# Attention scores by query: diagonal blocks in tiles of their own, one wide mask product per head, and the slots of a unit laid out anew

## The chip, the cores and the metric

The kernel runs as one program on one core of a Trainium2 chip. The time is device microseconds of one execution, median of several; lower is better. The engines are named as the profile names them: PE is TensorE's matmul row, PEld its weight loads, DVE is VectorE, ACT is ScalarE, POOL is GpSimd, SP issues the DMAs.

## The reference, cut to what matters

Six layers follow each other on x of 8 sequences x 512 positions x 128 features: a mixture of experts, an RWKV layer, the mixture again, a second mixture (top 1 of 8), causal attention, and the second mixture again. The change touches the attention alone:

```python
qkv = jnp.einsum('bsm,qhkm->qbhsk', x, w_qkv)          # 16 heads of 8
scores = jnp.einsum('bhsk,bhtk->bhst', Q, K) / sqrt(d_k)
scores = jnp.where(causal, scores, -jnp.inf)
probs = jax.nn.softmax(scores, axis=-1)
attn = jnp.einsum('bhst,bhtk->bhsk', probs, V)
x = x + einsum('bsd,md->bsm', attn_cat, w_o)
```

Here S is 512, in 4 blocks of 128.

## The kernel before, in words

The attention works through 8 sequences ("batches", functions `body(b, ...)`) of 4 units each. A unit (b, g) is 4 heads. Each head's q and k lie in 32 rows of a stack (`q_stack`, `k_stack`), so that a product of one head uses 32 of the 128 rows of PE, and products of different heads can run beside each other. The scores of a unit are computed twice:

- By query (`by_query`, PE lines 2019 and 2023), only to find each query's maximum. Six tiles n = 0..5 per unit, of two heads each, in PSUM banks 0 to 3, two tiles in flight. Before, a tile holds whole causal rows of a query block i: (i + 1) * 128 keys. Where the block touches the diagonal, a product of the identity with the constant `keys_after` (0 or -1e30, bf16, all 128 rows of PE, L2023) is added on its last 128 columns. n = 0, 1 hold block 3 (512 columns), n = 2, 3 hold block 2 (384) and block 0 (128), n = 4, 5 hold block 1 (256). DVE takes the maxima (`maxima`, L1490).
- By key (`by_key`, L2006), 12 tiles t = 0..11 per unit of one head each (t is called a slot), in banks 4 and 5 by turns: width 512 for t = 0..3, 384 for t = 4..7, 256 + 128 for t = 8..11. ACT takes their exponentials (`exps`, L938), POOL clears what lies beyond the diagonal (L620), and PE multiplies with the values one unit later (`weighted_values`, L2036, fp32, columns of PE in four groups of 32), in four parts j = 0..3 at slots 1, 3, 5, 5.

The maxima go by a transpose (`max_rows`, L1995), a copy on ACT (L945) and a DMA into the q stack of the unit, ahead of its by-key scores. `by_query` and `maxima` therefore run two units ahead of `by_key`.

The order on each engine is written out by hand in `body`: in each slot, weighted values, then `by_key(t)`, then in even slots `by_query(u + 2, ..., t // 2)`, then other work put at a slot: transposes of the weighted values (`transpose_values`, L2043, slot 8), which need ACT's copy `values` (L950); in unit g = 0 the projections of the next batch, `q_proj` at slot 6 and `k_proj` at slot 10 (L1590 to L1592, both into bank 7); `v_proj` in g = 1; in g = 2 `transpose_out` (L2049) at slot 6 and `out_proj` at slot 10, both in bank 7 too; in g = 3 the transposes of the next layer's input (L1580). `k_proj` waits for `q_low` of DVE (L1475), which waits for `q_high` of ACT (L925), since they empty bank 7. `out_proj` waits for `out_low` of DVE (L1507), which waits for `out_high` of ACT (L960), in the same way. `by_key(t)` waits for the exponential of slot t - 2 (semaphore `probs_ready`), `by_query(n)` for the maxima of tile n - 2 (`scores_by_query_used`).

## Time and profile before

| | |
|---|---|
| median of 3 runs | 1802.65 us (1800.73 to 1805.01) |
| the profiled execution | 1796.81 us, span 1794.7 us, mean granted clock 0.98 |
| attention | from 1374 to about 1715 us of the span |
| one batch of 4 units | 38.8 to 39.1 us where the clock stays up |
| PE busy, DVE busy over the span | 94%, 68% |

PE's busy time counts the whole latency of a matmul (a 128 column one is shown with 219 ns, though in a run of them one starts every 56 ns), so a busy PE may still be waiting in part. In the views of order of time, the first number is the start, the second the length of the group of like instructions, and a bracket tells the idle time before it and what ended it. A unit is found by its `by_key` matmuls of 512 columns on L2006.

### The profile page before, as it was taken

To read this page: it belongs to the slowest core of one execution; us is meant where nothing else is said; L and a number is where in the kernel's file an instruction comes from. 1 tells how busy PE (TensorE), PEld (TensorE's weight loads), DVE (VectorE), ACT (ScalarE), POOL (GpSimd) and SP (SyncE) were. 2 spreads that over 40 slices of the span, in tenths; PEclk is the share of its full clock that TensorE was granted. 3 is DMA by queue.
4 is the path that set the end of the run, shared out by engine and by line. 5 is a ranking of instruction groups with operands and counts; after the bars stand their busy time and mean duration, and the time that the engine had idled before them with its cause. 6 is when DMAs were issued, how large, how long until landed. Compare 5 with 4: busy or idle time off the path is not lost. (4 is left out here: it accounts for less than half of the span.)

```text
span 1794.7 us, 45173 instructions
## 1 busy us (share of the span) xinstructions
PE 1691.7 (94%) x15966; PEld 1000.2 (56%) x15966; DVE 1226.7 (68%) x2848; ACT 1017.1 (57%) x1956; POOL 876.7 (49%) x722
## 2 busy tenths in 40 slices
PE   7899999999998999979999999999999998999988
PEld 4566666666665666646666666666644343434334
DVE  5865666666667888746665665666678786888566
ACT  5655555555555566545555555566533775777633
POOL 2665765665541435556755655765443222232232
PEclk9999999999999999999999999999999998999889
DMA  4200000000000000000000000000001110111000
GB/s 144 85 20 1 0 0 0 0 0 1 2 1 2 2 0 0 2 1 1 2 1 0 0 0 0 0 1 1 2 1 25 28 37 15 43 28 25 2 13 35
DMA packets 14617, 23.41 MB, mean 13 GB/s; under 512 B 2570, under 2 KB 10890, under 8 KB 14356
## 3 DMA queue, kind: packets, MB, share of 16 engines
q1 hardware_dynamic: 14484, 21.62, 4.2%
q8 instruction: 85, 1.39, 0.3%
q14 instruction: 48, 0.39, 0.1%
HBM read 11.00 MB, written 2.10 MB: 7 GB/s over the span
## 5 line engine op out<-in xcount | busy, mean ns | idle before, releaser
L506 POOL TENSOR_TENSOR scratch<-scratch 128x512 f16<-128x512 f32 x384 | 445.5, 1160 | 416.6 <-ACT scratch L667 416.3
L667 ACT ACTIVATE scratch<-scratch 128x512 f16<-128x512 f32 x512 | 322.4, 630 | 440.7 <-DVE scratch L1110 440.6
L1110 DVE SCALAR_TENSOR_TENSOR scratch<-psum,scratch 128x512 f32<-128x512 f32 x512 | 352.9, 690 | 313.8 <-ACT scratch L662 180.1
L1628 PE MATMUL psum<-ffn_down_hi,scratch 128*128 128x128 f16 x2048 | 369.3, 219 | 2.5 <-POOL scratch L506 2.1
L1630 PE MATMUL psum<-ffn_down_hi,scratch 128*128 128x128 f16 x2048 | 369.2, 219 | 0.0
L1629 PE MATMUL psum<-ffn_down_lo,scratch 128*128 128x128 f16 x2048 | 369.2, 219 | 0.0
L662 ACT ACTIVATE scratch<-psum 128x512 f32<-128x512 f32 x512 | 296.7, 580 | 0.0
L1490 DVE TENSOR_REDUCE scratch<-psum 128x2 f32<-128x1024 f32 (+3 forms) x256 | 202.4, 822 | 56.7 <-PE psum L2023 53.5
L1628 PEld LDWEIGHTS psum<-ffn_down_hi,scratch 128*128 128x128 f16 x2048 | 200.3, 98 | 60.4 <-POOL scratch L506 3.1
L1629 PEld LDWEIGHTS psum<-ffn_down_lo,scratch 128*128 128x128 f16 x2048 | 200.4, 98 | 56.1
L1590 PE MATMUL psum<-x_hi,ffn_up_hi 128*128 (+1 forms) x512 | 195.7, 382 | 7.8 <-DVE scratch L1110 7.6
L1630 PEld LDWEIGHTS psum<-ffn_down_hi,scratch 128*128 128x128 f16 x2048 | 200.4, 98 | 0.0
L1590 PE MATMUL psum<-x_hi,ffn_gate_hi 128*128 (+1 forms) x512 | 194.7, 380 | 3.6 <-ACT scratch L662 2.7
L1591 PE MATMUL psum<-x_lo,ffn_up_hi 128*128 (+1 forms) x512 | 195.1, 381 | 0.0
L1592 PE MATMUL psum<-x_hi,ffn_up_lo 128*128 (+1 forms) x512 | 195.0, 381 | 0.0
L1591 PE MATMUL psum<-x_lo,ffn_gate_hi 128*128 (+1 forms) x512 | 194.8, 380 | 0.0
L1592 PE MATMUL psum<-x_hi,ffn_gate_lo 128*128 (+1 forms) x512 | 194.7, 380 | 0.0
L499 POOL TENSOR_TENSOR scratch<-e_const,scratch 128x16 f32<-128x16 f32 x56 | 163.4, 2917 | 0.0
L480 POOL TENSOR_TENSOR ln_rstd<-ln_var,neg_half 128x4 f32<-128x4 f32 x48 | 48.5, 1010 | 210.8 <-DVE ln_var L1030 210.8
L1125 DVE SCALAR_TENSOR_TENSOR x_tok<-psum,scratch,x_tok 128x128 f32 (+1 forms) x512 | 143.2, 343 | 5.3 <-DVE scratch L1100 2.9
L938 ACT ACTIVATE scratch<-psum 128x384 f32<-128x384 f32 x256 | 116.3, 490 | 43.0 <-PE psum L2006 41.7
L1117 DVE TENSOR_TENSOR scratch<-scratch 128x512 f16<-128x512 f32 x128 | 88.8, 694 | 52.6 <-ACT scratch L667 50.1
(225 smaller groups left out, 2861.6 us busy)
## 6 DMA issues: line engine op xcount, KB each, us to landing
raw<-in_ffn_w_dram SPq DMA_DIRECT2D x8, 768.0 KB, 4.5
scratch<-scratch SPq DMA_DIRECT2D x32, 128.0 KB, 2.7
ffn_up_hi<-scratch SPq DMA_DIRECT2D x32, 128.0 KB, 2.7
x_tok<-in_x_dram SPq DMA_DIRECT2D x8, 256.0 KB, 6.7
out_dram<-x_tok SPq DMA_DIRECT2D x8, 256.0 KB, 2.0
raw<-in_lin_dram SPq DMA_DIRECT2D x1, 1092.0 KB
half_sb<-in_half_dram SPq DMA_DIRECT2D x1, 544.0 KB, 5.7
con_sb<-in_con_dram SPq DMA_DIRECT2D x1, 410.5 KB, 5.1
```

The lines of the kernel that those rows point to most:

```text
L499: pool.tensor_tensor(lg_exp[:, c], e_const[:], lg_shift[:, c], ALU.pow).then_inc(s_exp, 1)
L506: pool.tensor_tensor(h_lo[r], h32[r], h_hi[r], ALU.subtract).then_inc(s_plo, 1)
L662: act.activation(gate_act[k % 2], bank(k % 2), ACT.Silu, scale=W_DOWN).then_inc(s_s, 1)
L667: act.activation(h_hi[k % HSLOTS], h32[k % HSLOTS], ACT.Copy).then_inc(s_hhi, 1)
L1110: dve.scalar_tensor_tensor(h32[k % HSLOTS], bank(5 + k % 2), W_DOWN, gate_act[k % 2], ALU.mult, ALU.mult).then_inc(s_h, 1)
L1490: ins = dve.tensor_reduce(neg_max[g % 2][:, a:a + SUB + 1:SUB], scores[:, :, at:at + (i + 1) * P], AX_X, ALU.max, negate=True)
L1590: pe.matmul(dst, lhs[0], rhs[0], start=first, stop=False)
L1591: pe.matmul(dst, lhs[0], rhs[1], start=False, stop=False)
L1592: return pe.matmul(dst, lhs[1], rhs[0], start=False, stop=last)
L1628: pe.matmul(dst, h_hi[r][:, cols], hi, start=k % FC == 0 and n == 0, stop=False, skip_group_check=True)
L1629: pe.matmul(dst, h_hi[r][:, cols], lo, start=False, stop=False, skip_group_check=True)
L1630: ins = pe.matmul(dst, h_lo[r][:, cols], hi, start=False, stop=k % FC == FC - 1 and n == SUB - 1, skip_group_check=True)
```

## The change

`by_query` now knows three kinds of tile. Kind 0 holds the four diagonal blocks of two heads: 8 products of 128 columns, and then one mask product of 512 columns per head, whose moving operand is `keys_after` repeated four times by a step of zero. Kinds 1 and 2 (`LEFT`) hold what lies left of the diagonal, without a mask: kind 1 block 3 (384 columns) and block 1 (128), kind 2 block 2 (256). The six tiles of a unit are of the kinds 2, 0, 1, 1, 0, 2.

DVE reduces a tile of kind 0 in one instruction (8 maxima of 128) into `neg_max`, the left parts into a new tile `neg_left`, and after the last tile takes the minimum of both for blocks 1 to 3 (negated maxima), with a semaphore `maxima_ready` that `max_rows` waits for.

In `body`, the weighted values stand at slots 1, 4, 6, 6 (before 1, 3, 5, 5). On ACT `values` moves from slot 6 to 7, `q_high` from 7 to 8, `v_copy` from 9 to 10, `out_high` from 7 to 8, the copy of the next input from 9 to 10. On PE `v_proj` and the next input's transposes move from slot 8 to 9; `transpose_values` stays at slot 8, `q_proj`, `transpose_out` at 6, `k_proj`, `out_proj` at 10.

```diff
@@ query_tile @@
-            return (2, 0)[n % 2], ([(3, 0)], [(2, 0), (0, 3 * P)], [(1, 0)])[n // 2]
+            return (2, 0)[n % 2], (2, 0, 1, 1, 0, 2)[n]
+
+        LEFT = {1: [(3, 0), (1, 3 * P)], 2: [(2, 0)]}
@@ ACT, body @@
-                            if t == 7 and g == 0 and more:
+                            if t == 8 and g == 0 and more:
                                 q_high(b + 1)
...
-                            if t == 6 and not (first and g == 0):
+                            if t == 7 and not (first and g == 0):
                                 values(u - 1)
-                            if t == 9 and g == 1 and more:
+                            if t == 10 and g == 1 and more:
                                 v_copy(b + 1, 1 - odd)
-                            if t == 7 and g == 2 and not first:
+                            if t == 8 and g == 2 and not first:
                                 out_high(b - 1)
...
@@ DVE, maxima @@
-                    for i, at in pieces:
-                        a = r * SUB + i
-                        ins = dve.tensor_reduce(neg_max[g % 2][:, a:a + SUB + 1:SUB], scores[:, :, at:at + (i + 1) * P], AX_X, ALU.max, negate=True)
+                    if kind == 0:
+                        ins = dve.tensor_reduce(neg_max[g % 2][:, r * SUB:(r + 2) * SUB], by(psum[...], 2 * SUB),
+                                                AX_X, ALU.max, negate=True)
+                    else:
+                        for i, at in LEFT[kind]:
+                            a = r * SUB + i
+                            ins = dve.tensor_reduce(neg_left[g % 2][:, a:a + SUB + 1:SUB], scores[:, :, at:at + i * P], AX_X, ALU.max, negate=True)
                     ins.then_inc(s_p1used, 1)
+                    if n == QT - 1:
+                        dve.wait_ge(s_p1used, QT * u + QT + 2)
+                        whole, left = [by(t, HG)[:, :, 1:SUB] for t in (neg_max[g % 2], neg_left[g % 2])]
+                        dve.tensor_tensor(whole, whole, left, ALU.min).then_inc(s_mneg, 1)
@@ PE, max_rows @@
-                    pe.wait_ge(s_p1used, QT * (u + 1) + 2)
+                    pe.wait_ge(s_mneg, u + 1)
@@ PE, by_query @@
-                    for m, (i, at) in enumerate(pieces):
+                    if kind == 0:
+                        for i in range(SUB):
+                            for x in range(2):
+                                rows, block = head(first + x), slice(i * P, (i + 1) * P)
+                                pe.matmul(bank(2 * (n % 2) + x)[:, block], q_stack[odd][g][rows, block], k_stack[odd][g][rows, block],
+                                          start=i == 0, stop=False, skip_group_check=True)
                         for x in range(2):
...
+                            ins = pe.matmul(by(bank(2 * (n % 2) + x), SUB), ident_b, keys_after.rearrange("p (o k) -> p o k", o=1).to_broadcast([P, SUB, P]),
                                             start=False, stop=True, skip_group_check=True)
+                    else:
+                        for i, at in LEFT[kind]:
+                            for x in range(2):
+                                rows = head(first + x)
+                                ins = pe.matmul(bank(2 * (n % 2) + x, at, at + i * P), q_stack[odd][g][rows, i * P:(i + 1) * P], k_stack[odd][g][rows, 0:i * P],
+                                                start=True, stop=True)
@@ PE, body @@
-                PV_AT = (1, 3, 5, 5)
+                PV_AT = (1, 4, 6, 6)
-                            if t == 8 and g == 1 and more:
+                            if t == 9 and g == 1 and more:
...
                                 v_proj(b + 1)
```

The places at which the order of the instructions counts are taken from batch 5, which is written out without a loop. Lines of the changed kernel are shifted: `by_key` is L2018 there, the diagonal blocks L2032, the wide mask L2035, the left parts L2041, weighted values L2054, `max_rows` L2007, `transpose_values` L2061, the projections L1602 to L1604.

PE, unit g = 0, slots 1 to 4, before:

```order
L2006 MATMUL psum<-ffn_up_hi 128x512 x2
L2019 MATMUL psum<-ffn_up_hi 128x512 x2
L2023 MATMUL psum<-big_sb 128x128 x2
L1995 MATMUL psum<-con_sb,scratch 16x128
L2036 MATMUL psum<-scratch,ffn_down_hi 32x384 x4
L2006 MATMUL psum<-ffn_up_hi 128x512
L2006 MATMUL psum<-ffn_up_hi 128x384
L2019 MATMUL psum<-ffn_up_hi 128x384 x2
L2019 MATMUL psum<-ffn_up_hi 128x128 x2
L2023 MATMUL psum<-big_sb 128x128 x4
```

The weighted values (j = 1) stand right behind full-width work, and slot 4 ends in masks. The same slots now:

```order
L2018 MATMUL psum<-ffn_up_hi 128x512 x2
L2032 MATMUL psum<-ffn_up_hi 128x128 x8
L2035 MATMUL psum<-big_sb 128x512 x2
L2007 MATMUL psum<-con_sb,scratch 16x128
L2018 MATMUL psum<-ffn_up_hi 128x512
L2054 MATMUL psum<-scratch,ffn_down_hi 32x384 x4
L2018 MATMUL psum<-ffn_up_hi 128x384
L2041 MATMUL psum<-ffn_up_hi 128x384 x2
L2041 MATMUL psum<-ffn_up_hi 128x128 x2
```

The masks of the unit's first half have gathered in slot 2, `by_key(3)` stands alone between them and the weighted values, and slot 4 has none.

PE, unit g = 0, slots 5 to 8, before (L1590 to L1592 are `q_proj`):

```order
L2006 MATMUL psum<-ffn_up_hi 128x384 x2
L2019 MATMUL psum<-ffn_up_hi 128x384 x2
L2019 MATMUL psum<-ffn_up_hi 128x128 x2
L2023 MATMUL psum<-big_sb 128x128 x4
L1590 MATMUL psum<-x_hi,scratch 128x512
L1591 MATMUL psum<-x_lo,scratch 128x512
L1592 MATMUL psum<-x_hi,scratch 128x512
L2006 MATMUL psum<-ffn_up_hi 128x384
L2006 MATMUL psum<-ffn_up_hi 128x256
L2006 MATMUL psum<-ffn_up_hi 128x128
L2019 MATMUL psum<-ffn_up_hi 128x256 x2
L2023 MATMUL psum<-big_sb 128x128 x2
```

Slots 6 to 8 now, with the transposes of the weighted values as the last row:

```order
L2018 MATMUL psum<-ffn_up_hi 128x384
L2041 MATMUL psum<-ffn_up_hi 128x384 x2
L2041 MATMUL psum<-ffn_up_hi 128x128 x2
L1602 MATMUL psum<-x_hi,scratch 128x512
L1603 MATMUL psum<-x_lo,scratch 128x512
L1604 MATMUL psum<-x_hi,scratch 128x512
L2018 MATMUL psum<-ffn_up_hi 128x384
L2018 MATMUL psum<-ffn_up_hi 128x256
L2018 MATMUL psum<-ffn_up_hi 128x128
L2032 MATMUL psum<-ffn_up_hi 128x128 x8
L2035 MATMUL psum<-big_sb 128x512 x2
L2061 MATMUL psum<-con_sb,scratch 128x128 x4
```

Slot 6 has lost its four masks, and slot 8 holds a whole diagonal tile with 1024 columns of mask.

DVE, unit g = 0 from its first maxima to `k_low` of g = 1 (L1475 is `q_low`, L1497 and L1501 are `normalise`), before:

```order
L1490 TENSOR_REDUCE scratch<-psum 128x2 x7
L1475 SCALAR_TENSOR_TENSOR scratch<-psum,scratch 128x512
L1497 RECIPROCAL scratch<-psum 128x16
L1501 TENSOR_TENSOR scratch<-psum,scratch 128x4x32
L1490 TENSOR_REDUCE scratch<-psum 128x2 x2
L1479 SCALAR_TENSOR_TENSOR scratch<-psum,scratch 128x512
```

And now:

```order
L1498 TENSOR_REDUCE scratch<-psum 128x2
L1493 TENSOR_REDUCE scratch<-psum 128x8
L1498 TENSOR_REDUCE scratch<-psum 128x2 x4
L1493 TENSOR_REDUCE scratch<-psum 128x8
L1478 SCALAR_TENSOR_TENSOR scratch<-psum,scratch 128x512
L1509 RECIPROCAL scratch<-psum 128x16
L1513 TENSOR_TENSOR scratch<-psum,scratch 128x4x32
L1498 TENSOR_REDUCE scratch<-psum 128x2
L1503 TENSOR_TENSOR scratch<-scratch 128x4x3
```

The reduction right ahead of `q_low` is now a diagonal one of 1024 elements instead of one of 512, and each unit ends with the minimum (L1503).

## Rows read from the trace of the kernel before

**Rows 1.** Busy time by window: length, busy (count) per engine, granted clock, DMA.

```profile
1552.00:1591.00 39.00, 35.74 (x379) 16.09 (x378) 32.17 (x59) 27.95 (x62) 10.93 (x17) 1.00 0.13 29
1484.90:1495.00 10.10, 10.10 (x65) 3.36 (x65) 5.37 (x9) 3.93 (x9) 1.25 (x3) 0.50 0.01 2
```

**Rows 2.** Who waited for whom, 1552 to 1591 us: total us, times, longest.

```profile
DVE scratch L1490 <- PE psum L2023: 5.8, 12, 0.7
...
PE psum L2006 <- ACT scratch L938: 3.4, 7, 0.8
```

**Rows 3.** Order of time on PE, unit g = 0, slots 0 to 6.

```profile
1551.74 0.38 PE L2006 MATMUL psum<-scratch 32*128 32x512 f16 x1 [0.54 <-ACT scratch L938]
...
1552.27 0.28 PE L2023 MATMUL psum<-big_sb 128*128 128x128 bf16 x2
1552.48 1.06 PE L2036 MATMUL psum<-ffn_gate_lo,ffn_down_lo 128*32 128x512 f32 x8
1553.48 0.39 PE L2006 MATMUL psum<-scratch 32*128 32x512 f16 x2
1553.49 0.59 PE L2019 MATMUL psum<-scratch 32*128 32x512 f16 x2
1554.01 0.29 PE L2023 MATMUL psum<-big_sb 128*128 128x128 bf16 x2
1554.14 0.27 PE L1995 MATMUL psum<-con_sb,scratch 128*16 128x128 f32 x1
1554.34 0.85 PE L2036 MATMUL psum<-scratch,ffn_down_lo 128*32 128x384 f32 x8
1555.12 0.39 PE L2006 MATMUL psum<-scratch 32*128 32x512 f16 x2
...
1555.99 0.86 PE L2036 MATMUL psum<-scratch,ffn_down_lo 128*32 128x256 f32 x16
1556.78 0.33 PE L2006 MATMUL psum<-scratch 32*128 32x384 f16 x2
1556.78 0.54 PE L2019 MATMUL psum<-scratch 32*128 32x384 f16 x4
```

**Rows 4.** PE, slots 8 to 11, and the starts of units g = 1, g = 2 and g = 0.

```profile
1558.73 0.61 PE L2043 MATMUL psum<-con_sb,scratch 128*128 128x128 f32 x4
...
1560.45 0.28 PE L2006 MATMUL psum<-scratch 32*128 32x256 f16 x1 [0.84 <-ACT scratch L938]
...
1560.87 0.38 PE L1590 MATMUL psum<-x_hi,scratch 128*128 x1
1561.09 0.38 PE L1591 MATMUL psum<-x_lo,scratch 128*128 x1
...
1561.62 0.39 PE L2006 MATMUL psum<-scratch 32*128 32x256 f16 x2
...
1571.89 0.38 PE L2006 MATMUL psum<-scratch 32*128 32x512 f16 x1 [0.54 <-ACT scratch L938]
...
1590.93 0.37 PE L2006 MATMUL psum<-ffn_up_hi 32*128 32x512 f16 x1 [0.63 <-ACT scratch L938]
```

**Rows 5.** Order of time on ACT, unit g = 0.

```profile
1557.15 0.87 ACT L938 ACTIVATE scratch<-psum 128x384 f32<-128x384 f32 x2 [0.48 <-PE psum L2006]
1557.90 0.60 ACT L950 ACTIVATE scratch<-psum 128x512 f32<-128x512 f32 x1
...
1559.00 1.01 ACT L925 ACTIVATE scratch<-psum 128x1024 f16<-128x1024 f32 x1
```

**Rows 6.** Order of time on DVE, units g = 0 and g = 2.

```profile
1560.04 0.69 DVE L1475 SCALAR_TENSOR_TENSOR scratch<-psum,scratch 128x512 f16<-128x512 f32 x1 [0.41 <-ACT scratch L925]
...
1579.85 0.68 DVE L1507 TENSOR_TENSOR scratch<-psum,scratch 128x512 f16<-128x512 f32 x1
```

**Rows 7.** Groups of DVE by shape: busy, mean ns.

```profile
L1490 DVE TENSOR_REDUCE scratch<-psum 128x2 f32<-128x1024 f32 x8 | 9.8, 1226 | 3.7 <-PE psum L2023 3.7
...
L1030 DVE TENSOR_SCALAR ln_var<-ln_mv 128x4 f32<-128x4 f32 x48 | 9.3, 194 | 3.6
```

More of the change, by code:

```diff
@@ L208, in build @@
         neg_max = [carve(HG * SUB) for _ in range(2)]
+        neg_left = [carve(HG * SUB) for _ in range(2)]
         max_row = carve(P, F16)
@@ L983, in body @@
                                 k_high(b + 1)
-                            if t == 6 and not (first and g == 0):
+                            if t == 7 and not (first and g == 0):
                                 values(u - 1)
-                            if t == 9 and g == 1 and more:
+                            if t == 10 and g == 1 and more:
                                 v_copy(b + 1, 1 - odd)
-                            if t == 7 and g == 2 and not first:
+                            if t == 8 and g == 2 and not first:
                                 out_high(b - 1)
-                            if t == 9 and g == 3 and prep:
+                            if t == 10 and g == 3 and prep:
                                 prep_xT(n0 + SUB * b + LEAD, (b + 2) % NB if isinstance(b, int) else b + 2, 7)
@@ L2010, in by_query @@
                 def by_query(u, b, g, n, odd):
-                    first, pieces = query_tile(n)
+                    first, kind = query_tile(n)
                     if n == 0:
@@ L2015, in by_query @@
                     pe.wait_ge(s_p1used, QT * u + n + 1)
-                    for m, (i, at) in enumerate(pieces):
-                        for x in range(2):
-                            rows = head(first + x)
-                            pe.matmul(bank(2 * (n % 2) + x, at, at + (i + 1) * P), q_stack[odd][g][rows, i * P:(i + 1) * P], k_stack[odd][g][rows, 0:(i + 1) * P],
-                                      start=m == 0, stop=False, skip_group_check=True)
-                    for m, (i, at) in enumerate(pieces):
-                        for x in range(2):
-                            ins = pe.matmul(bank(2 * (n % 2) + x, at + i * P, at + (i + 1) * P), ident_b, keys_after,
-                                            start=False, stop=True, skip_group_check=True)
+                    if kind == 0:
[4 more added lines that the diff above has]
+                                          start=i == 0, stop=False, skip_group_check=True)
+                        for x in range(2):
+                            ins = pe.matmul(by(bank(2 * (n % 2) + x), SUB), ident_b, keys_after.rearrange("p (o k) -> p o k", o=1).to_broadcast([P, SUB, P]),
+                                            start=False, stop=True, skip_group_check=True)
+                    else:
[4 more added lines that the diff above has]
+                                                start=True, stop=True)
                     ins.then_inc(s_p1, 1)
@@ L2122, in body @@
                                 out_proj(b - 1)
-                            if t == 8 and g == 3 and prep:
+                            if t == 9 and g == 3 and prep:
                                 if more:
```

6 lines of the change are left out of this document (4 added, 2 removed).

## The prediction

> **What bounds the kernel now.** I read the page first, for its span, the engines' shares and the slices that hold attention. The change touches attention only, so everything below is a sum over its 341 us. Then the windows: in 39 us, one batch of four units, PE is busy 35.7, DVE 32.2 and ACT 28.0 us, at the upper of the two clocks [rows 1]. The order of time on PE shows that no engine is the bound all the way. PE works in its written order and stops wherever its next product waits for an exponential: 3.4 us of modelled idle in 7 stops per batch behind ACT's main group [rows 2]. A stop costs more than that number. PE is counted busy for the latency of its last matmul: a 128 column product is shown with 0.22 us where the next could start after 0.055, so I add 0.15 us for each of the 7, and have about 4.4 us of waits and 34.7 us of work in a batch of 39.1. DVE is rarely the one that is waited for; it waits 5.8 us per batch for masks [rows 2]. So the change is worth what it takes from PE's 34.7 us of work, less what it adds to the 4.4 us of waits.
>
> **Prices, all from rows.** A 128 column product costs PE 0.055 us: two masks and then `max_rows` stand 0.13 apart [rows 3]. A 512 column product costs 0.22 (1560.87 to 1561.09, [rows 4]). Going from products on 32 rows to products on 128, or to the weighted values on 32 columns, costs an empty 0.10: the first mask starts 1552.27, the second 0.055 later would be through at 1552.38, and L2036 starts at 1552.48 [rows 3]. I call that a switch. Weighted values with the switch behind them: 1.00 for j = 0, 0.78 for j = 1, 0.79 for j = 2 and 3 (1552.48 to 1553.48, 1554.34 to 1555.12, 1555.99 to 1556.78, [rows 3]). Products of different heads run together, those of one head one after the other: L2006 and L2019 start 0.01 apart, and the masks behind them 0.52 later, twice 0.216 and a switch [rows 3]. An exponential of 384 columns starts 0.37 after its product (1556.78 to 1557.15) and takes 0.49 [rows 3, 5].
>
> The four diagonal blocks of a head are four weight loads and products one after the other in the same 32 rows. The trace's nearest case is slot 6: each of two heads does 384 and then 128 columns in its own rows, and all four are over in 0.54 us [rows 3], which is 0.16 for the product of `by_key` ahead of one of them, 0.16, 0.055 and the latency of 0.16, and leaves nothing for an exposed load. So I take 0.22 for the four blocks. The Trainium skill speaks against it: "TensorE: Matmul & The Clock Gate", Part 3, section The mechanism, says that a weight load overlaps running products only where its row group differs. By that rule each block after the first would wait for its load; the trace does not show it for two products in a row, and none here has four.
>
> **The work on PE, before and after.** The columns of a unit are the same: 5120 of scores, 2048 of masks. Masks in 4 products of 512 instead of 16 of 128 cost 0.86 us instead of 0.88. The switches of a unit are 15 before (six from row products into masks, six back, three from masks to weighted values) and 14 now (in and out of three places of weighted values, which stand between row products, and of four full-width ones): -0.10. The row products overlap better. Before, each mask cut them in six runs of 0.38, 0.43, 0.43, 0.38, 0.27, 0.27, 2.15 us. Now a unit g = 0 has 0.27, 0.43, 0.22, 0.22, 0.22, 0.38, 0.27 = 2.0, units without other work in slot 6 0.2 less. Together 0.3 to 0.5 us of work goes per unit, 1.65 us per batch: 33.0 us are left.
>
> **The waits, unit g = 0 of the changed order, from the start of `by_key(0)`.** Row products 0.22, switch, j = 0: `by_key(1)` at 1.31 and (3) at 2.48 after diagonal blocks (to 1.75), switch, masks 0.43, `max_rows` 0.11, switch. `by_key(4)` at 3.58, (6) at 4.68, `q_proj` 0.65 and two switches, (7) and (8) at 5.73. Until there nothing waits for over 0.1. The blocks and masks of slot 8 end at 6.64 and the transposes come next. They need `values`, which now stands behind the exponential of slot 7: product 5.73, exponential 6.10, `values` 6.48 to 7.08. Before, it was behind that of slot 6 and ended at 1558.50 against transposes at 1558.73 [rows 4, 5]. New wait 0.5. Transposes 0.44 and a switch: `by_key(9)`, (10) at 7.68, not waiting; here the 0.84 us stop before slot 10 is gone [rows 4]. They end at 7.95, `k_proj` is next. It needs `q_high` (1.01) and `q_low` (0.69) [rows 5, 6]. `q_high` follows the exponential of slot 8 and ends at 8.36, `q_low` 9.09. Before, `q_low` ended at 1560.73, and `k_proj` started at 1560.87 with no wait [rows 4, 6]. New wait 1.1. Then 0.65 and a switch, the unit ends at 9.9; before, 1551.74 to 1561.62, 9.9 too [rows 3, 4]. The other three by the same steps: g = 1 10.25 (before 10.27, to 1571.89), with 1.0 before slot 2 (ACT still does `k_high`, 1.0 us), 0.3 at the transposes, 0.5 before the next unit; g = 2 9.9, with 0.5 at the transposes and 1.25 before `out_proj`: DVE reaches `out_low` only after four long reductions and two normalisations, at 8.3, where it began 1579.85 before, 8.0 after the unit's start [rows 4, 6]; g = 3 9.3; these two before, 19.0 together, to 1590.93 [rows 4]. Sum 39.3 us, of which 6.3 are waits. Against 39.2 in the loop [rows 3, 4] and 38.8 in the written-out batches the change costs 0.1 to 0.5 us per batch: seven batches carry the projections, +2 us; the eighth, without them, loses the work and gains the transposes' wait, 0.
>
> **Small terms.** DVE does the same 5120 elements in the same 8 reductions per unit (1024 take 1226 ns, [rows 7]), whether in 2 or in 8 outputs. No row has 8 outputs of 128; between the same and a fixed part more (0.15 us, from 1226 less 1024 at 1.04 ns) I take the same. The minimum, 12 elements a row, has its nearest row in 4 elements at 0.19 us [rows 7]; with its wait for the reduction ahead it is 0.2 to 0.3 us per unit, behind tile 5, where the next tile's scores are late anyway; in g = 2 it is part of the DVE line ahead of `out_low`, counted above. Queued behind its wait is only the next reduction. `max_rows` needs it two microseconds into the next unit: no cost. The mask with a repeated operand has no row: between 0.22 (the 512 column row) and 0.38 (the whole length shown for it), I take 0.22, the distance of starts in a dense run. The first two units, before `by_key` runs, are bound by DVE: two minima more, 0.4 us, less 0.3 for a shorter first tile.
>
> Sum: +2 us on the profiled execution's 1796.8, 1798.8. The median of the runs is 5.8 above that execution, so 1804.5 is what I compare with 1802.65.
>
> **Rivals.** (1) *The waits don't grow*: ACT and DVE keep up, as `values` and the two high parts are 0.6 to 1.0 us pieces that could slide into gaps my steps do not see. Then 1.65 us of work goes per batch, or half of it: 8 batches, -6 to -13 us, 1790 to 1797. For it speaks that the 0.84 us stop at slot 10 goes and that DVE is not full; against it, that PE's waits before are exactly such short ends of ACT's queue. (2) *ACT's and DVE's pieces become the bound* at slots 8 to 10: if `q_low` and `out_low` come another 0.5 us later than I have them, since DVE now has a 1.23 us reduction directly ahead of both, each batch loses 1 us more, and the longer stops let the clock fall. A stretch of 10.1 us at the lower clock is there before, with PE busy throughout [rows 1]; the same work at twice the clock would be 5 us shorter, so one such stretch costs 4 to 5 us, and I count one or two more of them. Together +8 to +14, 1810 to 1817. It decides from the point at which the stop before `k_proj` passes 1.6 us. (3) *The diagonal tile is dearer on PE*: the four blocks of a head pair take the length shown for one 128 column product and more, or a mask product takes the whole 0.38 shown for L1590 [rows 4] instead of 0.22; +0.3 to +0.5 us in each of 64 diagonal tiles, half of it hidden by waits, +10 to +16, 1813 to 1819. The Trainium skill's rule above ("TensorE: Matmul & The Clock Gate", The mechanism) would be one way to it. (4) The clock goes the other way: masks now lie in two lumps next to the sparse slots, the stretch of 10 us at half clock does not come, -4 us, and the total falls to 1800.
>
> **How the numbers follow.** A run can tell 0.2%, 3.6 us, from no change. My own sum (0.36) gives 1801 to 1808, mostly within; rival 1 0.30, rival 2 0.20, rival 3 0.06, rival 4 0.08. Faster by over 0.2% comes from rival 1 and half of 4: 0.35. Slower from rivals 2 and 3 and a quarter of my own case: 0.34. Within: 0.31. The likeliest own range is 1801 to 1808; the range that takes in most of both sides is 1791 to 1815.
>
> **What would show it.** PE's L2061 with a stop of 0.3 to 0.5 behind ACT's `values` in every unit; the first of `k_proj` with about 1 us behind DVE L1478, the first of `out_proj` behind L1519; `by_key(10)` of g = 0 without its 0.84 us. PE's busy time in attention some 10 us lower. The reductions of 1024 at 1.23, the eight diagonal products over in 0.38 us, the two wide masks 0.22 apart. Batches of 39.3 us. If the stops at `k_proj` and `out_proj` are not there, batches take about 38 and rival 1 has it; if batches take 40 or more, rival 2.

## The result, and the profile after

The changed kernel takes 1819.01 us (median of 4 runs, 1811.78 to 1822.34) against 1801.69 of the kernel before in the same comparison: ratio 1.009, 95% interval 1.0054 to 1.0127. It is slower by some 17 us; the forecast was 1804.5 us with a range of 1791 to 1815. The profiled execution took 1811.78 us, 15.0 more than that of before; it is the fastest of the four, with a mean clock of 0.974 where their median is 0.968. Ratios and intervals in this document leave out two slow executions, one of `tiles_only` (7208.74 us) and one of `after_warm` (1828.90 us), which the medians still count.

From the page, the span and the first of its parts:

```profile
span 1810.0 us, 45237 instructions
...
PE 1689.0 (93%) x15966; PEld 996.0 (55%) x15966; DVE 1234.2 (68%) x2880; ACT 1022.0 (56%) x1956; POOL 876.8 (48%) x722
```

PE did as many instructions as before and was even busy 2.7 us less. The time is idle time and clock. The windows of a batch in the loop (first) and of one of the batches written out (second), and of 9.9 us late in attention; columns as in [rows 1]:

```profile
1557.54:1597.82 40.28, 34.72 (x382) 14.72 (x378) 33.27 (x63) 28.63 (x62) 10.93 (x17) 1.00 0.12 28
1597.82:1637.87 40.05, 34.30 (x382) 14.52 (x378) 33.24 (x63) 28.70 (x63) 10.93 (x17) 1.00 0.13 28
...
1698.10:1708.00 9.90, 8.60 (x55) 3.99 (x55) 1.50 (x5) 5.44 (x13) 1.27 (x2) 0.50 0.01 2
```

The kernel before, in the same batch of the loop and in the written-out batch behind the one above, both at the upper clock (the one above itself took 38.75 us before, PE busy for 35.40):

```profile
1552.25:1591.34 39.09, 35.83 (x380) 16.18 (x378) 32.27 (x58) 28.05 (x62) 10.88 (x17) 1.00 0.13 29
1630.09:1668.85 38.76, 35.41 (x380) 15.64 (x378) 32.18 (x58) 28.06 (x61) 10.93 (x18) 1.00 0.13 29
```

So a batch lost 1.11 us of PE's busy time (35.41 to 34.30) and is yet 1.2 to 1.3 us longer. What PE stood for, in that loop batch:

```profile
PE psum L2018 <- ACT scratch L941: 2.2, 4, 0.6
PE psum L1602 <- DVE scratch L1519: 1.3, 1, 1.3
PE psum L1602 <- DVE scratch L1478: 1.0, 1, 1.0
PE psum L2018 <- ACT ffn_gate_lo L941: 0.6, 1, 0.6
PE psum L2061 <- ACT scratch L953: 0.5, 2, 0.3
```

These add up to 5.6 us against 3.6 before (the 3.4 of [rows 2] and 0.2 behind exponentials in another buffer), and two of them, both at products behind DVE, are new and over a microsecond or near it. PE in order of time, written-out batch: rows of unit g = 0, the turns of the units, and g = 2 around `out_proj`. Line numbers are those of the changed kernel; L941 is the exponential on ACT:

```profile
1597.22 0.37 PE L2018 MATMUL psum<-ffn_up_hi 32*128 32x512 f16 x1 [0.61 <-ACT scratch L941]
...
1598.57 0.60 PE L2032 MATMUL psum<-ffn_up_hi 32*128 32x128 f16 x8
1599.10 0.60 PE L2035 MATMUL psum<-big_sb 128*128 128x512 bf16 x2
1599.54 0.27 PE L2007 MATMUL psum<-con_sb,scratch 128*16 128x128 f32 x1
...
1603.04 0.33 PE L2018 MATMUL psum<-ffn_up_hi 32*128 32x384 f16 x2
...
1604.44 0.65 PE L2061 MATMUL psum<-con_sb,scratch 128*128 128x128 f32 x4 [0.31 <-ACT scratch L953]
...
1606.47 0.39 PE L1602 MATMUL psum<-x_hi,scratch 128*128 128x512 f16 x1 [1.00 <-DVE scratch L1478]
...
1607.22 0.39 PE L2018 MATMUL psum<-ffn_up_hi 32*128 32x256 f16 x2
...
1617.64 0.37 PE L2018 MATMUL psum<-ffn_up_hi 32*128 32x512 f16 x1 [0.66 <-ACT scratch L941]
...
1623.57 0.40 PE L2032 MATMUL psum<-scratch 32*128 32x128 f16 x8
...
1627.01 0.23 PE L1602 MATMUL psum<-scratch 128*128 128x128 f16 x1 [1.25 <-DVE scratch L1519]
...
1627.78 0.39 PE L2018 MATMUL psum<-ffn_up_hi 32*128 32x256 f16 x2
...
1637.27 0.37 PE L2018 MATMUL psum<-scratch 32*128 32x512 f16 x1 [0.61 <-ACT scratch L941]
```

These answer to [rows 3, 4]. From one unit's start to the next: 10.00, 10.42, 10.14 and 9.49 us. Before, the same four took 9.76, 10.17, 9.30 and 9.52 (PE rows at 1590.93, 1600.69, 1610.86, 1620.16 and 1629.68 of its trace). In both kernels the rows that open g = 1 and g = 3 begin with the last product of slot 11, about 0.1 us ahead of the unit itself. Two thirds of the loss are in g = 2. The 0.84 us stop ahead of `by_key(10)` in g = 0 is gone [rows 4]. What `k_proj` and `out_proj` waited for, on ACT (L953 is `values`, L928 `q_high`, L963 `out_high`) and on DVE (L1493 reduces a diagonal tile, L1478 is `q_low`, L1519 `out_low`, L1503 the minimum), to set beside [rows 5, 6]:

```profile
1603.80 0.59 ACT L953 ACTIVATE scratch<-psum 128x512 f32<-128x512 f32 x1
...
1604.64 1.05 ACT L928 ACTIVATE scratch<-psum 128x1024 f16<-128x1024 f32 x1
...
1624.92 0.62 ACT L963 ACTIVATE scratch<-psum 128x512 f16<-128x512 f32 x1
```

```profile
1604.17 1.23 DVE L1493 TENSOR_REDUCE scratch<-psum 128x8 f32<-128x1024 f32 x1 [0.40 <-PE psum L2035]
1605.72 0.69 DVE L1478 SCALAR_TENSOR_TENSOR scratch<-psum,scratch 128x512 f16<-128x512 f32 x1 [0.32 <-ACT scratch L928]
...
1607.54 0.17 DVE L1503 TENSOR_TENSOR scratch<-scratch 128x12 f32<-128x12 f32 x1
...
1625.14 1.21 DVE L1493 TENSOR_REDUCE scratch<-psum 128x8 f32<-128x1024 f32 x1
1626.27 0.68 DVE L1519 TENSOR_TENSOR scratch<-psum,scratch 128x512 f16<-128x512 f32 x1
```

The two stops have different causes. In g = 0 DVE was through with its 1.23 us reduction at 1605.40 and waited 0.32 us for ACT's `q_high` (L928, ends 1605.69). In g = 2 ACT's `out_high` (L963) had ended at 1625.54, and DVE's `out_low` (L1519) stood behind the reduction until 1626.27: 0.7 us.

Where the 15.3 us of the two spans went, from the first exponential of each batch in the two traces: 1.4 ahead of attention, in code that is the same; 2.9 in attention's first steps, which ran 10.2 us at the lower clock (before: none); 5.6 in seven batches; 5.2 in the last one; 0.3 behind it. The half clock within attention, counted from its first product to the start of its last exponential, is 47.4 us, before 30.7. In the seven batches before had more of it (20.5 us against 13.7), so their difference at one clock is larger than 5.6, up to 7 times 1.25. In the last batch, which has no projections, the changed kernel had 23.5 us of half clock and before 10.2; its first two units, both at the upper clock, are no longer than before (17.48 against 17.55 us). So 8.1 of the 15.3 us lie in the first steps and the last batch, which together had 23.5 us more of half clock, and not in the seven batches with the new stops.

### The profile page after: what moved, and what is told of

Its sections match the earlier page's. It is cut to its first block and busy times, and to the rows that moved or that the text cites. A ratio compares the mean times of both kernels' runs of the same rounds, so it can differ in the third digit from the quotient of the medians.

```text
span 1810.0 us, 45237 instructions
## 1 busy us (share of the span) xinstructions
PE 1689.0 (93%) x15966; PEld 996.0 (55%) x15966; DVE 1234.2 (68%) x2880; ACT 1022.0 (56%) x1956; POOL 876.8 (48%) x722
## 5 line engine op out<-in xcount | busy, mean ns | idle before, releaser
L1602 PE MATMUL psum<-x_hi,ffn_up_hi 128*128 (+1 forms) x512 | 195.9, 383 | 6.6 <-DVE scratch L1113 6.3
L1602 PE MATMUL psum<-x_hi,ffn_gate_hi 128*128 (+1 forms) x512 | 195.0, 381 | 3.6 <-ACT scratch L665 2.7
L1604 PE MATMUL psum<-x_hi,ffn_gate_lo 128*128 (+1 forms) x512 | 195.0, 381 | 0.0
L1604 PE MATMUL psum<-x_hi,ffn_up_lo 128*128 (+1 forms) x512 | 194.7, 380 | 0.0
L941 ACT ACTIVATE scratch<-psum 128x384 f32<-128x384 f32 x256 | 122.0, 488 | 77.8 <-PE psum L2018 75.6
L1498 DVE TENSOR_REDUCE scratch<-psum 128x2 f32<-128x256 f32 (+1 forms) x192 | 125.5, 686 | 17.6 <-PE psum L2041 13.6
L623 POOL TENSOR_SCALAR_AFFINE_SELECT scratch<-scratch 128x512 f32<-128x512 f32 x96 | 59.4, 635 | 148.5 <-ACT scratch L941 148.5
```

The source lines that it names most:

```text
L1498: ins = dve.tensor_reduce(neg_left[g % 2][:, a:a + SUB + 1:SUB], scores[:, :, at:at + i * P], AX_X, ALU.max, negate=True)
L1602: pe.matmul(dst, lhs[0], rhs[0], start=first, stop=False)
L1604: return pe.matmul(dst, lhs[1], rhs[0], start=False, stop=last)
```

## The experiments

Two theories stood after the result. S: the later slots of ACT's pieces (`values`, `q_high`, `out_high`, one slot later than before) make the stops. T: DVE's long reduction of a diagonal tile, which now stands directly ahead of `q_low` and `out_low`, makes them. Beside them stands the clock: how much of the 17 us is half clock, and does that follow from the stops?

Since the clock differs from run to run, each line has two more columns beside the ratio. "Full-clock batch" is the sum over the four units of the shortest length of each, in the loop and written out, from the trace of one execution. "Clock" is the mean granted clock of the timed runs (median over them).

| kernel | median us | ratio to before, interval | clock | full-clock batch |
|---|---|---|---|---|
| before | 1798.7 to 1801.7 | | 0.977 | 39.04 / 38.75 |
| changed | 1819.01 | 1.009, 1.0054 to 1.0127 | 0.968 | 40.28 / 40.02 |
| `tiles_only` | 1801.45 | 1.002, 1.0000 to 1.0039 | 0.980 | 40.17 / 39.69 |
| `slots_only` | 1839.25 | 1.0223, 1.0195 to 1.0251 | 0.966 | 42.25 / 42.10 |
| `act_back` | 1814.67 | 1.0084, 1.0055 to 1.0112 | 0.968 | 39.49 / 40.35 |
| `light_last` | 1845.58 | 1.025, 1.022 to 1.028 | 0.968 | 43.17 / 43.11 |
| `light_last_old_slots` | 1811.87 | 1.0071, 1.0049 to 1.0093 | 0.968 | 38.85 / 38.37 |
| `out_low_first` | 1814.17 | 1.007, 1.0047 to 1.0093 | 0.972 | 40.14 / 39.80 |
| `act_back_warm` | 1806.09 | 1.002, 0.9999 to 1.004 | 0.975 | 39.77 / 39.30 |
| `after_warm` | 1808.58 | 1.0049, 1.0014 to 1.0083 | 0.976 | 40.27 / 40.01 |
| `light_last_warm` | 1792.11 | 0.9955, 0.9937 to 0.9973 | 0.982 | 38.76 / 38.33 |
| `before_warm0` | 1794.12 | 0.9963, 0.9945 to 0.998 | 0.981 | 39.04 / 38.72 |

(In both written-out batches of `act_back` some unit ran at half clock; its 40.35 isn't free of it.)

The clock column carries its own price. Over 22 runs of the kernel before (mean clock 0.974 to 0.982) the time falls 12.5 us per 0.01 of clock, correlation -0.94; over 12 runs of `light_last_warm` 11.9 us, -0.95. With that the table adds up: the changed kernel's 0.009 lower clock is 11 us, and brought to the clock of before it would stand at about 1808, 6 to 9 us above it, near the 8.8 us of seven batches that are 1.25 longer. This price is a correlation over executions; the runs with idle products below are what changes the clock on purpose.

**The change split in two.** `tiles_only` is the changed kernel with every slot as before; `slots_only` is the kernel before with the new slots:

```diff
 # tiles_only, against the changed kernel (ACT, then PE)
-                            if t == 8 and g == 0 and more:
+                            if t == 7 and g == 0 and more:
                                 q_high(b + 1)
-                            if t == 7 and not (first and g == 0):
+                            if t == 6 and not (first and g == 0):
                                 values(u - 1)
-                            if t == 8 and g == 2 and not first:
+                            if t == 7 and g == 2 and not first:
                                 out_high(b - 1)
...
-                PV_AT = (1, 4, 6, 6)
+                PV_AT = (1, 3, 5, 5)
```

(`v_copy`, `prep_xT`, `v_proj` and `prep_transpose` go back by one slot too.)

> The new tiles (diagonal blocks apart, wide mask, minimum) with every slot as before (weighted values 1, 3, 5, 5; ACT's values 6, q_high and out_high 7). Batches without half clock take 38.8 us before and 40.05 us changed. Theory S, the later slots of ACT make PE's stops at k_proj and out_proj: a batch near 38.8 (38.4 to 39.1), the stop before k_proj under 0.3 us, total 1798 to 1806. Theory T, the 1.23 us reduction of a diagonal tile that now stands right ahead of q_low and out_low on DVE makes them: a batch of 39.5 to 40.0, the stop before out_proj still over 0.8 us, total 1808 to 1816.

> The old tiles with every slot as in the changed kernel. Theory S: a batch of 39.8 to 40.3 us, the stops before k_proj (1.0) and out_proj (over 0.9) as in the changed kernel, total 1810 to 1820. Theory T: a batch of 38.9 to 39.4, since the reduction ahead of q_low and out_low is the short one of 512 elements again, total 1801 to 1809.

Measured: 1801.45 and 1839.25 us. The tiles by themselves lengthen a full-clock batch by 0.9 to 1.1 us, the slots by themselves by 3.2 to 3.4, both together by 1.25: the slots were fitted to the tiles, but weren't better than the old ones even with them. `tiles_only` met the time that theory S gave and nearly the batch that theory T gave; `slots_only` came out above both bands. PE's stops in the written-out batch, `tiles_only` and then `slots_only` (which has the line numbers of the kernel before: L2043 the transposes, L950 `values`, L1590 `k_proj`, L1475 `q_low`):

```profile
1606.79 0.39 PE L1602 MATMUL psum<-x_hi,scratch 128*128 128x512 f16 x1 [0.44 <-DVE scratch L1478]
```

```profile
1616.70 0.66 PE L2043 MATMUL psum<-con_sb,scratch 128*128 128x128 f32 x4 [0.74 <-ACT scratch L950]
...
1618.72 0.39 PE L1590 MATMUL psum<-x_hi,scratch 128*128 128x512 f16 x1 [0.78 <-DVE scratch L1475]
```

With the new tiles and the old slots the stop at `k_proj` is 0.44 (`out_proj`'s 0.95), with the old tiles and the new slots 0.78 (0.35). Theory S has the greater part of `k_proj`'s stop, theory T of `out_proj`'s; neither has both. `slots_only` also has the transposes of each unit wait 0.6 to 0.7 for `values` and PE busy for 37.2 us against 35.4. `tiles_only` also stands 4.0 us ahead of `by_key` products in that batch, before 3.2, which neither theory names. It stands only 3 us above before in spite of seven batches that are 1 us longer; its clock, 0.980 against 0.977, is worth the rest by the price above. So its hit on the time of theory S was luck of the clock.

**ACT's pieces back in their old slots**, PE left as changed:

```diff
-                            if t == 8 and g == 0 and more:
+                            if t == 7 and g == 0 and more:
                                 q_high(b + 1)
-                            if t == 7 and not (first and g == 0):
+                            if t == 6 and not (first and g == 0):
                                 values(u - 1)
-                            if t == 8 and g == 2 and not first:
+                            if t == 7 and g == 2 and not first:
                                 out_high(b - 1)
```

> The changed kernel with only ACT's values, q_high and out_high one slot earlier (6, 7, 7 as before); PE's and DVE's orders are the changed ones. Theory S: a batch of 38.8 to 39.3 us, stop before k_proj under 0.3, before out_proj under 0.5. Theory T: q_low ends no earlier than the reduction ahead of it allows, a batch of 39.6 or more.

Measured: 1814.67 us, a batch 0.8 us shorter (39.49), the transposes without a stop, `k_proj` at 0.46. But `out_proj` rose to 1.45, and the half clock in attention is 79 us in the profiled execution. `out_proj` has that stop in six batches, and in five of them a stretch at the lower clock begins in it or at most 1.1 us behind it. Here the products of `out_proj` start 0.07 and 0.05 apart, then 0.08 to 0.11:

```profile
1631.25 0.23 PE L1602 MATMUL psum<-scratch 128*128 128x128 f16 x1 [1.45 <-DVE scratch L1519]
1631.32 0.23 PE L1603 MATMUL psum<-scratch 128*128 128x128 f16 x1
1631.37 0.28 PE L1604 MATMUL psum<-scratch 128*128 128x128 f16 x1
1631.45 0.31 PE L1602 MATMUL psum<-scratch 128*128 128x128 f16 x1
1631.56 0.31 PE L1603 MATMUL psum<-scratch 128*128 128x128 f16 x1
```

S is right on the 0.8 us, though not on `out_proj`, whose stop was to be under 0.5. The timed runs have the same clock as the changed kernel, 0.968, and are 4.3 us faster, not far from what 0.8 us in seven batches give. The profile of the changed kernel is of an execution with 0.974, so 47 and 79 us of half clock overstate how far the two kernels differ.

**The short tiles last.** The order of the query tiles by kind is changed (0 is the diagonal tile with a 1.23 us reduction, 1 has two reductions that take 1.28 together, 2 one of 0.69), so that DVE has a short one ahead of `q_low` and `out_low`. The diagonal tiles come to slots 4 and 6. `light_last` keeps the new slots, `light_last_old_slots` has the old ones:

```diff
-            return (2, 0)[n % 2], (2, 0, 1, 1, 0, 2)[n]
+            return (2, 0)[n % 2], (1, 1, 0, 0, 2, 2)[n]
```

> The changed kernel with the tiles in the order of kinds 1, 1, 0, 0, 2, 2, so that DVE's reduction ahead of q_low and out_low is the short one of 512 elements (0.69 us) and the long ones come earlier; all slots as changed. Theory S: q_low still waits for q_high, the stop before k_proj stays near 1.0 us and a batch at 39.6 to 40.1. Theory T: the stop before out_proj falls from 1.25 to under 0.7 and a batch to 39.3 or less.

> The changed kernel with its kinds of tiles in the order 1,1,0,0,2,2 (the diagonal-by-query group last among the light ones) and every slot as it was before the change. Theory T (the 1.23 us reduction of the diagonal group stands right ahead of q_low and out_low on DVE): with the group moved to the end of the unit, the stops at k_proj and out_proj fall to about 0 and at most .2 us, a full-clock batch is at most 39.0 us, time 1790 to 1800 us. Theory S (it is ACT's later slots that make the stops): old slots take them away too, k_proj under .3, but out_proj keeps about .9 as with the tiles alone; batch 39.7, time about 1801. If slot 8's transposes still wait for `values` as in the run with this order and the new slots (.96 each), batch above 40.5 and time above 1805.

(The second text words the order loosely: the tiles that come last are the short ones, not the diagonal ones.)

Measured, `light_last`: 1845.58 us, batch 43.1, both far above what either theory gave. `out_proj`'s stop fell from 1.25 to 0.57, as T has it, but `k_proj`'s stayed at 1.00, and with nothing long in slot 8 the transposes stand 0.96 us for `values`, in every unit:

```profile
1634.54 0.66 PE L2061 MATMUL psum<-con_sb,scratch 128*128 128x128 f32 x4 [0.96 <-ACT scratch L953]
...
1636.56 0.39 PE L1602 MATMUL psum<-x_hi,scratch 128*128 128x512 f16 x1 [1.00 <-DVE scratch L1478]
```

With the old slots every one of these stops is gone (`k_proj`, `out_proj` and the transposes follow on PE without idle time), and a batch takes 38.85 in the loop and 38.37 written out: 0.2 to 0.4 us less than in the kernel before. So the diagonal tile is a gain in itself, where its reduction is ahead of nothing that PE waits for and ACT's pieces keep their slots. The time, however, is 1811.87 us, 12 above the upper end of T's forecast, and the windows of one loop batch and one written-out batch say why:

```profile
1557.65:1602.66 45.01, 40.94 (x382) 17.38 (x378) 32.82 (x62) 28.14 (x62) 10.88 (x17) 0.85 0.11 25
1642.57:1680.95 38.38, 34.28 (x382) 15.31 (x378) 32.66 (x62) 28.14 (x62) 10.94 (x18) 1.00 0.13 29
```

Nearly the same work (38.85 us at full clock in the loop) takes 45.0 us at a mean clock of 0.85 and 38.4 at 1.00. This kernel's batches 2 and 4 fall to half clock twice each, batch 3 once apart from the turn of the loop, batch 1 not at all. PE stood 1.0 us in two stops in a row shortly ahead of such a fall (this one at 1582.35):

```profile
1579.46 0.33 PE L2018 MATMUL psum<-scratch 32*128 32x256 f16 x2 [0.47 <-ACT scratch L941]
1580.34 0.39 PE L2018 MATMUL psum<-scratch 32*128 32x512 f16 x1 [0.54 <-ACT scratch L941]
```

**`out_low` ahead of the long reduction**, everything else as changed:

```diff
+                            if n == 4 and g == 2 and not first:
+                                out_low(b - 1)
                             ... # maxima of tile n
-                            if n == 4 and g == 2 and not first:
-                                out_low(b - 1)
```

> The changed kernel with out_low on DVE put ahead of the maxima of tile 4 in group 2, so that it doesn't stand behind their 1.23 us reduction. Theory T: the stop at out_proj falls from 1.25 to about .55 us, batch at full clock 40.3 -> 39.7 to 40.0, time 1805 to 1812 us. Theory S: out_proj's stop is set by ACT's out_high and stays above 1.0 us; time as the changed kernel, 1812 to 1819 us.

Measured: 1814.17 us. On DVE:

```profile
1624.48 0.69 DVE L1519 TENSOR_TENSOR scratch<-psum,scratch 128x512 f16<-128x512 f32 x1 [0.36 <-ACT scratch L963]
1625.09 1.22 DVE L1493 TENSOR_REDUCE scratch<-psum 128x8 f32<-128x1024 f32 x1
```

and on PE:

```profile
1625.23 0.23 PE L1602 MATMUL psum<-scratch 128*128 128x128 f16 x1 [0.57 <-DVE scratch L1519]
```

The stop is 0.57, as T gave it, and now ACT's `out_high` sets it. The time is above T's band. By the shortest lengths in the loop, unit g = 2 went from 10.37 to 9.68 us, but g = 3 from 9.33 to 9.87; a batch gains 0.1 to 0.2. The trace shows where it went. PE at the start of g = 3, and DVE's `normalise`, for which the weighted values wait:

```profile
1626.45 0.28 PE L2041 MATMUL psum<-scratch 32*128 32x256 f16 x2
1626.84 1.07 PE L2054 MATMUL psum<-ffn_gate_hi,ffn_down_lo 128*32 128x512 f32 x8
...
1626.50 0.29 DVE L1513 TENSOR_TENSOR scratch<-psum,scratch 128x128 f32<-128x128 f32 x1
```

The long reduction now ends 1626.31, and the tile that waits for it starts 0.45 us behind `by_key`, which starts 1626.00. `normalise` follows it on DVE and ends 1626.79, and the first weighted values start 0.84 us behind `by_key`; in the changed kernel that distance is 0.37 (1627.78 to 1628.15). PE's busy time hides most of this, since it counts the latency of the products ahead. T is right on the stop, but DVE's queue is the limit on both sides of it: what `out_proj` gained, the next two pieces of DVE took back. The rest of the 5 us is clock (0.972 against 0.968).

**Is the half clock a consequence of the stops?** The stops are filled with idle products of 128 columns, written to a bank that nobody reads at that time. They compute nothing that is used:

```diff
+                def warm(n, u):
+                    pe.wait_ge(s_p1used, QT * (u + 2) + QT + 1)
+                    for _ in range(n):
+                        pe.matmul(bank(0, 0, P), ident16, ident16, start=True, stop=True)
...
+                                warm(14, u)      # ahead of k_proj
...
+                                if more:
+                                    warm(10, u)  # ahead of out_proj
```

> The run with ACT's pieces back in their old slots (1814.7 us, 79 us of half clock inside attention, one stretch of 3.4 us in nearly every batch, at the out_proj stop), with idle matmuls of 128 columns put in the stops: 14 ahead of k_proj in group 0, 10 ahead of out_proj in group 2, into a bank that nobody reads then. If the half clock comes from the stops, the stretches go (half clock in attention 10 to 35 us instead of 79) and the time falls to 1795 to 1806 us, batches 39.2 to 39.6. If it comes from elsewhere, the half clock stays at 60 to 90 us and the time at 1812 to 1822 us.

> The changed kernel with the same idle matmuls in its k_proj and out_proj stops (.99 and 1.25 us). If part of its loss is half clock that follows from the stops, the half clock in attention falls from 47 us to 10 to 35 and the time from 1818 to 1806 to 1813 us, with full-clock batches still at 40.2. If the stops have no part in the half clock, 45 us or more of it stay, and the time is 1815 to 1825 us.

Measured: 1806.09 against 1814.67 us, and 1808.58 against 1819.01; mean clock 0.968 to 0.975 and 0.976. The second time lies in the band for "the half clock comes from the stops", the first 0.1 us above its own (1795 to 1806). The half clock in the one profiled execution does not: 69 and 43 us, where 10 to 35 was expected. The profiled execution of `act_back_warm` is the slowest of its ten, with a clock of 0.968 against their median of 0.975. The half clock is gone from the batches where the stops were filled, as in this batch of `act_back` and then of `act_back_warm`:

```profile
1602.79:1643.41 40.62, 35.42 (x382) 15.46 (x378) 33.07 (x63) 28.75 (x63) 10.98 (x17) 0.96 0.12 28
```

```profile
1605.45:1644.84 39.39, 35.15 (x406) 16.25 (x402) 33.06 (x63) 28.74 (x63) 10.96 (x17) 1.00 0.13 29
```

What is left lies in attention's first steps, the first batch, around the loop's branch and in the last batch, which the products reach partly or not at all. The full-clock batch of `after_warm` is that of the changed kernel (40.27 and 40.28), so its gain is clock and nothing else. At `out_proj` PE still stands 0.65 us (0.85 in `act_back_warm`) ahead of the idle products, which wait for the same reduction; in these two traces no fall followed on that shorter stop. The answer is yes for the middle batches, and no more than that.

The same for the pair of stops at the turn of the units, in `light_last_old_slots` and, to know what it brings by itself, in the kernel before. The wait of `warm` is one unit earlier there, since it stands ahead of slot 0:

```diff
+                            if t == 0 and more and follows:
+                                warm((9, 0, 9, 0)[g], u)
                             by_key(u, b, g, t, odd)
```

> The kernel with the diagonal-by-query group last and all old slots (1811.9 us; full-clock batches 38.85 and 38.38, but 51 us of half clock in attention, six of its seven falls in the loop 1 to 2 us behind a pair of stops of .47 and .54 us at by_key(11) and by_key(0) of groups 3 and 1), with nine idle matmuls of 128 columns ahead of by_key(0) in groups 0 and 2, where PE stands for .63 us. If the falls come from the two stops in a row, the half clock between the first and the last exp falls from 51 to under 25 us, batches at full clock stay under 39.0, and the time is 1792 to 1800 us, at or below that of the kernel before. If they don't, the half clock stays over 40 us and the time at 1808 to 1815.

> The kernel before with the same nine idle matmuls ahead of by_key(0) in groups 0 and 2, to tell what they bring by themselves: before shows 31 us of half clock in attention, of it 10 at the loop's branch and 10 in the last batch, which they can't reach. If they do nothing else, 1796 to 1803 us; a gain of 2 to 5 us if the remaining 10 us of half clock go; 1804 or more if they delay by_key, whose stop of .63 us they fill to .5.

Measured: 1792.11 and 1794.12 us, 0.4% below the kernel before each, with intervals that overlap (0.9937 to 0.9973 and 0.9945 to 0.998). PE at the turn of a unit in `light_last_warm` (L2104 are the idle products), where `light_last_old_slots` had its two stops:

```profile
1609.56 0.33 PE L2018 MATMUL psum<-ffn_up_hi 32*128 32x256 f16 x2 [0.47 <-ACT scratch L941]
1609.83 0.68 PE L2104 MATMUL psum<-half_sb 128*128 128x128 f16 x9
1610.52 0.37 PE L2018 MATMUL psum<-ffn_up_hi 32*128 32x512 f16 x1
```

and its batches, to set beside the two windows above:

```profile
1552.06:1591.05 38.99, 36.07 (x400) 16.79 (x396) 32.80 (x62) 28.16 (x61) 10.91 (x17) 1.00 0.13 29
1629.42:1668.12 38.70, 34.85 (x391) 15.79 (x387) 32.65 (x62) 28.16 (x61) 10.97 (x18) 1.00 0.13 30
```

The loop batch is 6.0 us shorter than in `light_last_old_slots`, and the half clock between the first and the last exponential fell from 51 to 10 us, in `before_warm0` from 31 to 7. With attention's first steps counted, in which both profiled executions had half clock and their counterparts had none, it is 51 to 24 and 31 to 17. `before_warm0` gained 6 us where I expected 0 to 5. `light_last_warm` is faster than both kernels of this case; most of that comes from the idle products, and its own 0.3 us per batch (2 to 3 us in all) is shown by the traces and not by the medians, which are 2 us apart.

## Why the prediction was wrong

Rival 2 comes nearest to what happened, with its size at 17 us where I had put 8 to 14, and my own case with its "+0.1 to +0.5 us per batch" failed. Batches of 40 or more were to be its sign, and they are 40.0 to 40.3. Its reason came only in part: `q_low` and `out_low` were to be another 0.5 us late, and the start of `k_proj` was 0.2 late and that of `out_low` 0.3; the stop at `k_proj` was 1.0, not over 1.6.

**Prices.** Those in doubt were right. The reduction with 8 outputs takes 1.21 to 1.23 us, the minimum 0.17. The eight diagonal products are over in 0.40 us (row 1623.57) and 0.38 was given; so rival 3 is out. The two wide masks take 0.44 up to the start of `max_rows` (1599.10 to 1599.54), that is 0.22 each. The Trainium skill's rule that a weight load overlaps running products only where its row group differs ("TensorE: Matmul & The Clock Gate", Part 3, The mechanism) did not hold here: four loads in a row in the same 32 rows, of two heads side by side, left no gap to be seen in those 0.40 us.

**Unit g = 0** came out as worked out, step by step: `by_key(3)`, `(6)`, `(7)` and the transposes were forecast at 2.48, 4.68, 5.73 and 7.14 us behind the unit's start and came at 2.5, 4.7, 5.8 (1603.04) and 7.2 (1604.44); `k_proj` at 9.05 and 9.25; the end at 9.9 and 10.0 written out, 10.2 in the loop. The stop at the transposes (0.3, forecast 0.5), the one at `k_proj` (1.0 shown and 0.15 of latency, forecast 1.1), and the stop that goes, are there.

**The step that failed** is the difference of work and waits, "33.0 us are left" and "Sum 39.3 us, of which 6.3 are waits", and with it the clock, which my own case left where it was. Work: 1.65 us was to go per batch, 1.11 went. Waits: they were to grow by 1.9, and grew by 2.4 (5.75 against 3.35 us shown, in 11 stops each in the written-out batch). Both missed by 0.5 us in the same direction, and a difference of two terms of 1.7 to 1.9 cannot take that. I had worked only g = 0 out slot by slot and given the other three "by the same steps" in a line, and there most of the error is: written out, the four units took 0.10, 0.17, 0.24 and 0.19 us more than forecast. The largest, g = 2, was to take 9.9 and takes 10.14 written out and 10.3 in the loop. Its `out_proj` stop is 1.25 shown, 1.40 with the latency, where I had 1.25 in all: `out_low` began 8.6 us behind the unit's start, not 8.3. And g = 1 has a stop of 0.52 at 16.8 us of the batch, g = 3 one at 36.6, that stand in no step of mine: there `by_key(8)` waits for the exponential of slot 6. Per batch the cost was 1.25 us in place of 0.1 to 0.5; over seven batches that is 5 to 8 of the 14.5 us by which 1804.5 was missed.

**The clock** I had as a term of rival 2, one or two more stretches of 10 us. The profiles show 16.7 us more half clock, at 12.5 us per 0.01 of the mean clock some 6 us; the timed runs show 0.009 less clock, 11 us. Rival 4 had the time fall by 4 us, and it rose; whether masks in lumps keep the clock up by themselves stays open. The 10 us stretch of before is not in the changed kernel's profile, and `tiles_only`, with the same lumps, has a clock of 0.980; no run separates lumps from stops. Here my own case was at fault in principle: I had forecast a batch with 6.3 us of waits in place of 4.4 and left its clock where it was.

**The chances.** I had put 0.34 on slower. Rivals 2 and 3 reached to 1817 and 1819, and my range stopped at 1815. A wider bound was in reach: the median of before is itself 5 to 6 us above its own profiled execution, and 4 of them are clock by the price above (0.980 against 0.977).

## What to carry to other kernels

Where PE follows a written order and the gain is a difference between work taken off and waits added, work every unit out slot by slot, and widen the range by the sum of both errors. Ahead of a piece on DVE or ACT for which PE waits, put the shortest item of that queue, not the longest, and see what stands behind it in the same queue; after each edit look at the stops that remain one after the other, as they cost clock beyond their length. Compare two kernels at equal clock (full-clock stretches of the trace) before an edit is judged by its median: here `light_last_old_slots` had batches 0.2 to 0.4 us shorter and was 10 us slower.

## What the runs showed of the hardware

- Half clock followed on stops in a stage in which PE is 90% busy: of the 18 falls from the first exponential to the last batch, without those at the loop's branch, in the traces of before, changed, `act_back` and `light_last_old_slots`, 17 came where PE had just been idle for 1.0 to 1.5 us (one stop of 0.9 to 1.45, alone or with a shorter one ahead of it, or two of 0.5 to 0.7 in a row); the other came behind 0.5 us. Such stops do not always bring a fall: in batches 1 to 6 of the changed kernel they stand in 12 places, `k_proj` and `out_proj` of each, and 2 of them were followed by one; in `act_back` it was 5 of 6 at `out_proj`. What decides between them the runs don't show. Nine idle products of 128 columns in such a place, in two of four units, took 6 us off a kernel of 1800 us.
- A microsecond at half clock goes with about a third of a microsecond of time in the timed runs of this kernel: 0.01 of mean clock is 36 us at half clock in 1800, and 12 us of time. In attention single traces show a little more: the batch of `light_last_old_slots` with 13.7 us of half clock is 6.2 us longer than at full clock (45.01 against 38.85), and units g = 2 and g = 3 of batch 4 of `act_back`, with 3.4, are 1.5 us longer (21.02 against 19.51).
- A reduction of 1024 elements takes 1.21 to 1.23 us with 8 outputs per row as with 2 [rows 7].
- Two successive stops of PE of 0.5 us, whose filling makes a batch hardly shorter at full clock (38.85 against 38.76 us), were yet worth up to 20 us of total time through the clock (1811.87 against 1792.11).
- Attention's first steps held a stretch of 10 to 14 us at half clock in some executions and not in others of kernels with the same code there: none in the profile of before, 10 us in that of `before_warm0`. The edit may still have a part in it: all six profiled kernels with the changed order of the tiles (changed, `tiles_only`, `act_back`, `out_low_first` and the two with idle products) have such a stretch, and of the other six only `before_warm0` and `light_last_warm`. One execution of each does not settle it.
